# Two transformer layers on one core: values of the second attention one unit later, and a first attention, a feed-forward start and a layer norm put in another order

## The reference

```python
xn = _layernorm(x, axis=-1)
x = x + _L0_attn_ref(xn, ...) + _L0_ffn_ref(xn, ...)
xn = _layernorm(x, axis=-1)
x = x + _L1_attn_ref(xn, ...) + _L1_ffn_ref(xn, ...)
# L0 attention: 16 heads of 32, 4 key heads, full softmax over 1024 keys
# L0 feed-forward: silu(x W1^T) * (x W3^T), Walsh-Hadamard over 2048, then W2
# L1 attention, 16 heads of 2 x 64, window of 128 keys:
diff = jax.nn.relu(a1 - lam[None, :, None, None] * a2)
diff = diff / (jnp.sum(diff, axis=-1, keepdims=True) + 1e-06)
out = jnp.einsum('bhqk,bhkd->bhqd', diff, v)
# L1 feed-forward: a shared expert, and 32 experts of which 4 take a token (at most 64 tokens each)
```

## Time and profile before

| what | us |
|---|---|
| median of 3 runs | 2681.59 |
| the profiled execution | 2685.59 |
| its span | 2683.8 |
| PE busy in the span | 2520.4 (94%) |
| DVE, ACT, POOL busy | 1739.0, 1113.2, 1023.7 |
| mean granted clock of PE | 0.976 |

### The profile page before, as it was taken

One profiled execution on the slowest core, in us unless ns is written; L12 is line 12 of the kernel. 1 busy time (PEld: TensorE's weight loads), 2 busy tenths in 40 slices (PEclk: granted clock), 3 DMA queues, 4 the chain that ended last, 5 costly groups with the idle time before them and its releaser, 6 DMA issues. The chain is left out here.

```text
span 2683.8 us, 35815 instructions
## 1 busy us (share of the span) xinstructions
PE 2520.4 (94%) x12212; PEld 1691.8 (63%) x12212; DVE 1739.0 (65%) x3811; ACT 1113.2 (41%) x2809; POOL 1023.7 (38%) x757
## 2 busy tenths in 40 slices
PE   6899999999699999999789999979999889999998
PEld 3444444443278888887566777657777656657886
DVE  6677676665245555555648999949999823335886
ACT  1246555555223333232316777707777611111111
POOL 2348777776311111110006767615454410002442
PEclk9989999999799999999899999999999999999999
DMA  4721221202300000000312100010000098873101
GB/s 173 242 50 32 49 56 25 56 13 89 131 32 16 16 16 16 16 1 0 103 55 75 44 21 21 21 47 17 17 9 8 1 324 294 290 280 92 48 25 63
DMA packets 153639, 193.64 MB, mean 72 GB/s; under 512 B 52622, under 2 KB 98702, under 8 KB 153088
## 3 DMA queue, kind: packets, MB, share of 16 engines
q1 hardware_dynamic: 141952, 178.90, 21.0%
q0 software_dynamic: 11520, 12.64, 1.5%
HBM read 161.95 MB, written 54.53 MB: 81 GB/s over the span
## 5 line engine op out<-in xcount | busy, mean ns | idle before, releaser
L725 DVE TENSOR_REDUCE neg<-bank 128x1 fp32r<-128x1024 f32 x256 | 300.8, 1213 | 146.9 <-PE bank L629 146.8
L775 ACT ACTIVATE probs<-bank 128x512 f32<-128x512 f32 x512 | 289.5, 596 | 253.8 <-PE bank L639 237.4
L569 POOL TENSOR_TENSOR probs<-probs 128x1024 f32<-128x1024 f32 x128 | 301.5, 2376 | 172.5 <-PE bank L648 172.5
L1579 POOL TENSOR_SCALAR mix<-mix,sm 128x256 f32<-128x256 f32 (+1 forms) x256 | 232.6, 919 | 174.6 <-DVE sm L1477 174.3
L1520 ACT ACTIVATE ms<-ms,sm 128x256 f32<-128x256 f32 (+1 forms) x512 | 247.6, 486 | 112.5 <-DVE sm L1448 111.6
L639 PE MATMUL bank<-q_parts,k_parts 97*128 97x512 f32 x512 | 203.1, 444 | 1.7 <-ACT probs L775 0.7
L947 POOL TENSOR_TENSOR up_lo<-up_raw,up_hi 128x1024 fp32r<-128x1024 f32 x16 | 46.1, 2903 | 403.1 <-ACT up_hi L937 403.1
L1448 DVE CUSTOM_DVE_ANT_0 ms<-bank,misc 128x256 f32<-128x256 f32 (+1 forms) x512 | 184.8, 400 | 2.4
L629 PE MATMUL bank<-k_parts,q_parts 96*128 96x512 f32 x512 | 176.6, 433 | 6.9 <-DVE neg L725 4.9
L639 PEld LDWEIGHTS bank<-q_parts,k_parts 97*128 97x128 f32 x512 | 87.1, 189 | 146.3 <-ACT probs L775 122.9
L1017 DVE TENSOR_TENSOR hid<-bank,sg 128x512 f32<-128x512 f32 x64 | 44.3, 692 | 180.8 <-ACT sg L967 180.8
(11 more groups left out here) (227 smaller groups left out, 5874.2 us busy)
## 6 DMA issues: line engine op xcount, KB each, us to landing
ewg<-in_L_ffn_Wg_dram SPq DMA_DIRECT2D x32, 704.0 KB, 6.6
ewu<-in_L_ffn_Wu_dram SPq DMA_DIRECT2D x32, 704.0 KB, 7.9
ewd<-in_L_ffn_Wd_dram SPq DMA_DIRECT2D x32, 512.0 KB, 5.3
q_parts<-qk_dram SPq DMA_DIRECT2D x48, 256.0 KB, 4.3
up_raw<-in_L_ffn_W_dram SPq DMA_DIRECT2D x16, 512.0 KB, 4.4
ewd<-in_L_ffn_Wd_dram SPq DMA_DIRECT2D x32, 192.0 KB, 5.7
qk_dram<-qk_hi SPq DMA_DIRECT2D x20, 256.0 KB, 2.2
qk_dram<-qk_lo SPq DMA_DIRECT2D x20, 256.0 KB, 2.0
```

Source lines behind the costliest of these rows:

```text
L569: pool.tensor_tensor(probs[:, even, half, :], probs[:, even, half, :], probs[:, odd, half, :], ALU.add).then_inc(S["paired"], 1)
L725: dve.tensor_reduce(neg[:, U % HPT, q:q + 1], bank[:, 2 * (n % 2):2 * (n % 2) + 2, :], AX.XY, ALU.max, negate=True).then_inc(S["max"], 1)
L775: act.activation(probs[:, s % BUFS, j, :], bank[:, 4 + j % 2, :], ACT.Exp, scale=scale).then_inc(S["exps"], 1)
L1579: pool.tensor_scalar(mix[:, p % 2, h, 0:w], mix[:, p % 2, h, 0:w], sm[:, p % 3, 8 + h:9 + h], None, ALU.mult).then_inc(S["probs"], 1)
```

## The change

Five parts.

A. `heads0`: on PE, `peaks` comes before `score` 0, and `sums` stands right ahead of `values`. The weight is mixed in 8 parts of 64 columns instead of 4 of 128, in four quarter buffers, so that each `mix` has half the elements; there are 16 for a part, as before, a part now goes over 7 pairs instead of 14, and its fetch and store move half the bytes in pieces of half the length. In the last turn the reciprocals, the scaling and the projection follow each other by quarters.

B. `swiglu`: PE waits for each split weight where it uses it; the first G rows of the second weight are loaded ahead of the rest; ACT splits the weights ahead of the second chunk of tokens. The second layer norm's moments are taken chunk by chunk in the last pass of DVE's additions.

C. `layer_norm` and `route` become one block, `normalise_and_route`: a chunk's router logits stand between the transposes of the next chunk; the low part of the value weights on POOL waits until the rows are nearly done; the values use two banks.

D. `project_keys_values` counts those value weights in four steps (KD - 1 more).

E. `attention1_heads`: `weigh` goes one step later and to the place right behind `turn`, `project` and `add` one step later with it; `values_low` moves ahead of the second mask.

```diff
-CW = P
+CW = 64
...
-    PERIOD, PARTS0 = 14, D // CW
+    PERIOD, PARTS0, LATER = 7, D // CW, 5
...
-                        if j < PARTS0 and m:
-                            for n in range(16 * (m - 1) // (PERIOD - 1), 16 * m // (PERIOD - 1)):
+                        if j < PARTS0:
+                            for n in range(16 * m // PERIOD, 16 * (m + 1) // PERIOD):
                                 mix(16 * j + n)
...
-                        score(V, s, 0)
                         if not projects:
                             peaks(n)
+                        score(V, s, 0)
                         score(V, s, 1)
...
+                        if s % 2 and N > 1:
+                            sums(N // 2 - 1)
                         if N:
                             values((N - 1) // QB, (N - 1) % QB)
                         score(V, s, 2)
                         score(V, s, 3)
-                        if s % 2 and N > 1:
-                            sums(N // 2 - 1)
...
-            sp.dma_start(wd[:, :, :], down).then_inc(ready, 16)
+            sp.dma_start(wd[:, 0:G, :], down[:, 0:G, :]).then_inc(env["fw"]["got"], 16)
+            sp.dma_start(wd[:, G:, :], down[:, G:, :]).then_inc(ready, 16)
...
-                if c == 0 and h == 0:
-                    wait(pe, S["split"], i * 6 + 3 * a + 3)
...
                 for m in range(2):
+                    if c == 0 and h == 0:
+                        wait(pe, S["split"], i * 6 + 3 * a + m + 1)
...
         tokens_high(act, 0)
+        high(act, 0, 0, G)
         tokens_high(act, 1)
-        high(act, 0, 0, G)
...
+                if last and a == 1:
+                    for s in range(SUBS):
+                        wait(dve, S["added"], (i * 2 + a) * (NC * SUBS) + c * SUBS + s + 1)
+                        dve.bn_stats(stats[:, s, :], X[:, c * SUBS + s, :]).then_inc(env["ln"][0], 1)
...
                 for c in range(NC):
+                    for s in range(SUBS):
+                        turn_rows(c * SUBS + s)
+                        if c and s == 1:
+                            logits(c - 1)
+                        if c and s == 3:
+                            turn_logits(c - 1)
+                logits(NC - 1)
+                values(0)
+                turn_logits(NC - 1)
...
+                pool.wait_ge(xn_ready, 2 * NT - 1)
+                for k in range(KD):
+                    pool.wait_ge(H["khi"], CREDIT + k + 1)
+                    pool.tensor_tensor(wvl[:, k, :], wv[:, k, :], wvh[:, k, :].bitcast(F32), ALU.subtract).then_inc(H["klo"], 1)
...
-        for s in range(UNITS + 4):
+        for s in range(UNITS + 5):
             if s + 1 < UNITS:
                 scores(s + 1)
             if 3 <= s < UNITS + 3:
                 turn(s - 3)
+            if 4 <= s < UNITS + 4:
+                weigh(s - 4)
             if s // 4 + AHEAD < CHUNKS:
                 queries(s // 4 + AHEAD, s % 4)
-            if 3 <= s < UNITS + 3:
-                weigh(s - 3)
-            if s >= 4:
-                project(s - 4)
+            if s >= 5:
+                project(s - 5)
...
             if 2 <= s < UNITS + 2:
                 invert(s - 2)
+            if 5 <= s < UNITS + 5:
+                values_low(s - 5)
             if s < UNITS:
                 mask(s, 1)
-            if s >= 5:
-                add(s - 5)
-            if 4 <= s < UNITS + 4:
-                values_low(s - 4)
+            if s >= 6:
+                add(s - 6)
```

More of the change, by code:

```diff
@@ L499, in heads0, with buf @@
         probs = sb(ctx, "probs", [P, 4, HPT, CH])
-        both = sb(ctx, "w2_parts", [P, 2 * HT0 * CW])
-        bufs = [both[:, m * HT0 * CW:(m + 1) * HT0 * CW].rearrange("p (h n) -> p h n", n=CW) for m in range(2)]
+        both = sb(ctx, "w2_parts", [P, 4 * HT0 * CW])
+        quarters = [both[:, m * HT0 * CW:(m + 1) * HT0 * CW].rearrange("p (h n) -> p h n", n=CW) for m in range(4)]
+        def buf(j, away):
+            return quarters[2 * (j % 2) + (j // 2 + away) % 2]
         ring = both[:, :].rearrange("p (r h n) -> p r h n", r=RING, n=D)
@@ L572, in norm @@
                 def norm(V):
-                    row = oT[:, V % (KD + 1), :]
-                    wait(pool, S["rec"], V + 1)
                     wait(pool, S["o_taken"], V + 1)
-                    pool.tensor_tensor(row, row, den[:, :], ALU.mult).then_inc(S["normed"], 1)
+                    for part in range(SUBS if V == TURNS - 1 else 1):
+                        cols = slice(part * P, (part + 1) * P) if V == TURNS - 1 else slice(0, CH)
+                        row = oT[:, V % (KD + 1), cols]
+                        wait(pool, S["rec"], V + 1 + part)
+                        pool.tensor_tensor(row, row, den[:, cols], ALU.mult).then_inc(S["normed"], 1)
                 def mix(n):
@@ L580, in mix @@
                     h = 1 << st
-                    src, dst = (bufs[(j + st + m) % 2].rearrange("p (g two h) n -> p g two h n", two=2, h=h) for m in range(2))
+                    src, dst = (buf(j, st + m).rearrange("p (g two h) n -> p g two h n", two=2, h=h) for m in range(2))
                     if n % 16 == 0:
                         wait(pool, F["got"], 16 * (j + 1))
-                        wait(pool, F["stored"], 16 * j)
+                        wait(pool, F["stored"], 16 * (j - 1))
                     if k == 0:
@@ L900, in down @@
                 wait(pe, S["parts"], i * (PER * NC) + n + 1)
+                if c == 0 and h == 0:
+                    wait(pe, S["split"], i * 6 + 3 * a + 3)
                 if h == 0:
@@ L939, in high @@
         if isinstance(number, int) and number == 0:
+            wait(act, env["fw"]["got"], 16 * (D // CW + 1))
+        else:
             act.wait_ge(ready, ready_value)
@@ new lines, in logits @@
+                def logits(c):
+                    if c == 0:
+                        pe.wait_ge(router_high, 4)
+                    pe.wait_ge(xt_taken, NT + SUBS * (c + 1))
+                    pe.wait_ge(lgT_s, c)
+                    for k in range(KD):
+                        for part, (w, x) in enumerate(((wrh, xh), (wrh, xl), (wrl, xh))):
+                            mm = pe.matmul(bank[:, 3, :], w[:, k, :], x[:, k, c * CH:(c + 1) * CH],
+                                           start=(k == 0 and part == 0), stop=(k == KD - 1 and part == 2))
+                    mm.then_inc(lgT, 1)
@@ new lines, in turn_logits @@
+                def turn_logits(c):
+                    pe.wait_ge(lgT_s, c + 1)
+                    for s in range(SUBS):
+                        n = c * SUBS + s
+                        mm = pe.transpose(bank[:, 4 + c // 2, (n % 8) * W:(n % 8 + 1) * W],
+                                          logT[:, s * P:(s + 1) * P], ident[0:W, 0:W])
+                    mm.then_inc(lg, 1)
+                def values(n):
+                    if n == 0:
+                        pe.wait_ge(H["khi"], CREDIT + KD)
+                    pe.wait_ge(H["vtaken"], CREDIT + n - 1)
+                    for part, (x, w) in enumerate(((xh, wvh), (xl, wvh), (xh, wvl))):
+                        for k in range(KD):
+                            if n == 0 and part == 2:
+                                pe.wait_ge(H["klo"], CREDIT + k + 1)
+                            mm = pe.matmul(bank[:, 6 + n % 2, :], x[:, k, n * P:(n + 1) * P], w[:, k, :],
@@ L1495, in _ @@
                 turn_queries(c, a)
-        for s in range(UNITS + 5):
+        for s in range(UNITS + 6):
             if s < UNITS:
```

305 lines of the change are left out of this document (156 added, 149 removed).

## The result

The changed kernel takes 2650.47 us (median of 4 runs, 2649.03 to 2652.47), against 2681.83 of the kernel before: a ratio of 0.9883, interval 0.9869 to 0.9897. The forecast was 2649, with a range from 2630 to 2668. The total was nearly right, but two of its terms were wrong by 17 and 19 us in opposite directions. So the stages tell more than the sum.

What follows compares the result with a forecast made beforehand. PE was taken as the bound in the long stages. Terms -9.7 - 2.3 - 10.8 - 11.8 + 2 = -32.6 took 2685.6 to 2653.0 us profiled, 2649 us as a median, range 2630 to 2668.

Steps and rivals of the forecast that it cites:

- A, the steps: First attention: fewer switches into and out of narrow products save 0.18 us in each of 54 pairs, -9.7 us.
- A, the end: End of first attention: projection starts 3.3 us earlier by quarters, last POOL sum comes 1.0 later, -2.3 us (0 to -3.3).
- B: Start of first feed-forward: first products need only the first half of the up weight's low part, -10.8 us (-8 to -12).
- C: Layer norm and router ahead of the values: three gains less +9.0 for logits between transposes, -11.8 us (-3 to -17).
- the +9.0 for logits between the transposes: Layer norm and router: three chunks of 12 matmuls at half clock, 5.2 us each, lengthen the rows by about 3.0 each.
- the three gains: Layer norm and router: earlier first row -6.6, POOL's low part no longer slowing a row tile -2.9, logits ahead of values -11.3.
- E: Second attention: waits for `pt` go, against longer drains and 2.5 us lost in each group, +2 us (-18 to +12).
- the rule: Second attention: `invert`, slowed beside POOL's rotation, delays `values_low` and `weigh`; all 20 us at stake lost, 2667, chance 0.05.
- third rival: Second attention: late `pt` goes round a ring of relu, `invert`, `values_low`, `weigh`; 47 us lost, 2696, chance 0.04.
- rival 1: Second attention: every wait for `pt` goes and no new one comes, -18 instead of +2, 2629, chance 0.12.
- rival 2: First attention: POOL becomes the bound if half-sized `mix` costs as much as full, 2683; milder, switches bring nothing, 2659; chance 0.11.
- rival 4: Layer norm and router: transposes and logits block each other on PE at half clock, C gives -3, 2658, chance 0.06.

Runs made afterwards that it cites:

- e_one_input: Changed kernel with `invert`'s first operation written as two 128x1 operations, each with one tensor input and a scalar operand: 2642.67 us, ratio 0.9846.
- e_ot_early: Changed kernel with `values_low` ahead of `invert` on DVE and the copy `oT_hi` ahead of the relu on ACT: 2629.42 us, ratio 0.9798.
- c_low_early: Changed kernel without the wait that holds POOL's low part of the value weights until the rows are nearly done: 2651.24 us, ratio 0.9879.

## Why the prediction was right, and where it was wrong

**The total** was right within 2 us because two misses, A by -17 and E by +19, cancel; that is luck. The mechanisms of B and C, and the bound by PE, hold. Two of the signs that the prediction named did not come: a pair takes 7.06 us and not 7.3 to 7.45, and each group of the second attention is some 10.5 us longer and not within 6.

**A, the steps** (-9.7, measured -25.0): what failed is the step "I take the value near the switch". The prediction named the other end, 30 us if putting `peaks` first removes every wait for exponents, and gave it no weight, since no row in its list priced it. The price of the switches had the right size: 0.18 us a pair were counted, and moving `sums` gives 0.10 with `peaks` at their old place and 7.35 - 7.07 = 0.28 with `peaks` first. But `peaks` first is worth 0.25 us alone and 0.43 with `sums` moved, and that was at nothing. The steps show it: one without `sums` falls from 3.33 to 3.10 us by `peaks` alone, and one with `sums` falls from 4.27 to 3.99 only by both (4.20 and 4.25 by `sums` and `peaks` alone). The profile of the kernel before had a hint: the scores' weight loads stood for 122.9 us behind ACT's exponents (84.4 in the changed kernel).

**A, the end** (-3.3 without the sums, measured -4.3) and **B** (-10.8, measured -10.9): right; as shown above, the gap ahead of the projection fell by 3.1, and the rest lies within what the projection varies by. For B the row of `up_lo` named the moment to 0.1 us, which is closer than the 9.4 to 10.5 us of the runs lets one expect.

**C** (-11.8, measured -14.2): the gains came about as worked out. To the first row it is 1235.29 - 1227.95 from the last additions, where it was 1285.30 - 1271.06: -6.9 instead of -6.6; ahead of the values stand 2.9 us of logits (1260.29 to 1263.18) instead of 14.1. What was mis-sized is the +9.0 for logits between the transposes, of which some 6 came: up to the first value product 14.6 us are saved, and the three gains make between 20 and 21. The clock was back at its higher level by the first of them, behind transposes from 1235.86 on: 12 matmuls from 1241.60 to 1244.48, 0.24 each and not 0.43, at a granted clock of 1.00, which it kept to 1264; in the kernel before, the pitch of 0.43 stood at a clock of 0.50 (from 1307 to 1309). By the prediction's own sum that would leave 3 x (2.9 - 2.1) = 2.3. What it left out is PE's wait for ACT's copy of the logits ahead of turning them, 1.21, 1.73 and 1.21 us.

**E** (+2, ends -18 and +12; measured +20.9, beyond both ends): the sign was right and the size wrong. The drains cost what was said (3.9 for 4), and the steps without queries gave back 4.3 us of the 7 counted. The steps with queries, for which 2.5 us a group were counted, took 10.7 us a group. Two steps failed.

The first is "`weigh` comes only behind the scores and transposes, about 1.5 us after the masks can start, and little of it shows". In the step shown above PE was free at 1423.47 - 0.40 = 1423.07, and `values_low` ended only at 1422.92 + 0.40 = 1423.32. In 26 such steps PE stood for 13.8 us of the 20 named, and without the block 8 us come back (`e_one_input`). The prediction had the row, 0.87 against 0.16, and the 20 us at stake, and kept the case in which all of them are lost, 2667 ("the rule" in its range), apart from the sum, at a chance of 0.05. That E then lost 21 us, about those 20, is chance: the block made up some 8 of them, and the rest came by other ways.

The second is the price of 2.5 us a group for the steps in which a weight is split and while the pipe fills. In those steps, and in the drains, the copy `oT_hi`, last on ACT, held `values_low`. `weigh` had to wait for `values_low` before too, but stood behind the queries; ahead of them the wait shows. `e_ot_early` got 9 us back. The prediction looked at the late `pt` and the relu (third rival). The relu does hold `invert`, and so `values_low` (6.2 us in ten waits), but the late `pt` stays in `e_ot_early`, where E costs nothing any more.

**Rivals.** E's full gain did not come, as new waits took the place of those for `pt`. POOL did not become the bound of the first attention. Of the third rival's ring, the links from the relu to `invert`, `values_low` and `weigh` are there; the late `pt`, which was to close it, was not needed for the loss, and 47 us did not come. C did more than said. The forecast had a chance of 0.62, with a spread of 2638 to 2660, rival 1 0.12, rival 2 0.11 (0.03 near no change, 0.08 in its milder form), rival 3 0.04 and rival 4 0.06.

## What to carry to other kernels

When a product is moved earlier on the engine that sets the pace, list everything its new place now waits for, in the order of each feeding engine, and move those operations with it: here `weigh` moved, with `values_low` left behind `invert` and `oT_hi` last on ACT, and lost 21 us; with these two moved ahead as well it lost nothing. Ask first whether work that is there anyway can fill the wait; projecting before weighing did, for one edit on one engine. And when a total agrees with the forecast, compare the stages: two errors of 17 and 19 us were hidden in a sum that was right within 2.

## What the runs showed of the hardware

`invert`, a VectorE operation on 128x2 elements with two tensor inputs from SBUF, takes 0.15 to 0.16 us with no GpSimd operation beside it and 0.81 to 1.13 us beside the first of the rotation's two, of 1.3 us (28 cases in the changed kernel); the same sum as operations on 128x1 with one tensor input and a scalar operand takes 0.19 to 0.21 us each beside it (`e_one_input`, 56 cases). A 128x512 normalisation with one tensor input, two scalar operands and an SBUF output, 0.54 us alone, took 0.91 to 1.53 us beside GpSimd's low part of the value weights (`c_low_early`, four rows; those operations take 1.3 to 1.5 us), and 3.43 us beside the one of 4.51 us in the kernel before. So the number of tensor inputs alone doesn't say which operation waits, and no run here shows what does.
